# A two-layer graph network kernel: set-up and loop in one block, weights folded by whole fp32 products

## The reference, cut to what matters

```python
# x [128, 128, 256] f32, adj [128, 128, 128] int
h = relu(layernorm(x));  A = (adj != 0)
for i in range(3):                      # a gated graph layer, weights shared but for weight[i]
    m = h @ weight[i]                   # [256, 256]
    aggr = einsum('bst,bsd->btd', A, m)
    gi = aggr @ w_ih.T + b_ih           # w_ih, w_hh [768, 256]
    gh = h @ w_hh.T + b_hh
    r, z = sigmoid(i_r + h_r), sigmoid(i_z + h_z)
    n = tanh(i_n + r * h_n)
    h = (1 - z) * n + z * h
x = x + h
h = relu(layernorm(x))
Wh = h @ W.T;  s1 = Wh @ a1;  s2 = Wh @ a2      # attention layer
att = softmax(where(adj == 0, -inf, leaky_relu(s1[:, :, None] + s2[:, None, :])))
out = x + att @ Wh
```

## Time and profile before

| what | value |
|---|---|
| median of three runs | 1756.61 us |
| the profiled execution, its own time | 1757.19 us |
| its span, first to last instruction | 1755.4 us |
| PE busy | 1737.4 us, 99% |
| DVE busy | 1491.1 us, 85% |
| ACT busy | 1104.0 us, 63% |
| POOL busy | 312.2 us, 18% |
| first gate product on PE | 36.22 us |

### The profile page before, as it was taken

How to read it: one execution, slowest core, us unless ns; L and a number is a source line. 1 busy time by engine, 2 the same in 40 slices (tenths; PEclk the granted TensorE clock), 3 DMA queues, 4 the chain that set the end, 5 groups by cost and what they waited for, 6 DMA issues and landing times. The chain is left out here.

```text
span 1755.4 us, 32032 instructions
## 1 busy us (share of the span) xinstructions
PE 1737.4 (99%) x10108; PEld 906.8 (52%) x10108; DVE 1491.1 (85%) x2916; ACT 1104.0 (63%) x2005; POOL 312.2 (18%) x759
## 2 busy tenths in 40 slices
PE   7999999999999999999999999999999999999998
PEld 5444555545555454554545555455554545545455
DVE  6578898888988888888888988889888888888888
ACT  5456666666566666666666666665666666666664
POOL 1022022210212112021120222102121120211200
PEclk9999999999999999999999999999999999999999
DMA  4334352354424444253343523444244342533332
GB/s 116 71 61 103 59 133 55 72 119 89 114 42 103 94 84 108 42 120 87 74 114 62 129 54 74 117 90 114 42 106 91 84 108 42 120 88 73 79 67 67
DMA packets 395712, 152.03 MB, mean 87 GB/s; under 512 B 307360, under 2 KB 391840, under 8 KB 395680
## 3 DMA queue, kind: packets, MB, share of 16 engines
q1 hardware_dynamic: 395680, 151.64, 38.4%
HBM read 60.83 MB, written 16.84 MB: 44 GB/s over the span
## 5 line engine op out<-in xcount | busy, mean ns | idle before, releaser
L1162 ACT ACTIVATE n_out<-n_pre,bih 128x512 f32<-128x512 f32 x192 | 137.8, 718 | 191.7 <-DVE n_pre L1286 190.8
L551 ACT ACTIVATE nb_hi<-nb_bank 128x512 f16<-128x512 f32 x192 | 114.0, 594 | 217.4 <-PE nb_bank L537 217.4
L522 PE MATMUL hn_bank<-ht_s,wh_hi 128*128 128x512 f16 x768 | 228.4, 379 | 1.7 <-PEq L637 1.7
L522 PE MATMUL z_bank<-ht_s,wh_hi 128*128 128x512 f16 x768 | 228.4, 379 | 0.0
L522 PE MATMUL r_bank<-ht_s,wh_hi 128*128 128x512 f16 x768 | 228.4, 379 | 0.0
L1157 ACT ACTIVATE tanh_r<-r_bank,b_rz,down 128x512 f32<-128x512 f32 x192 | 148.5, 773 | 113.1 <-PE r_bank L522 113.1
L1281 DVE SCALAR_TENSOR_TENSOR n_pre<-tanh_r,hn_b 128x512 f32<-128x512 f32 x192 | 147.6, 769 | 79.2 <-ACT tanh_r L1157 77.0
L555 DVE TENSOR_TENSOR nb_lo<-nb_bank,nb_hi 128x512 f16<-128x512 f32 x192 | 131.1, 683 | 49.5 <-ACT nb_hi L551 49.5
L1529 POOL TENSOR_TENSOR ht<-ht_s 128x512 f32<-128x512 f16 x64 | 86.0, 1345 | 468.7 <-DMA ht_s<-h_s 350.5
L1152 ACT ACTIVATE hn_b<-hn_bank,b_hn,down 128x512 f32<-128x512 f32 x192 | 147.8, 770 | 19.0 <-PE hn_bank L522 18.9
L1166 ACT ACTIVATE tanh_z<-z_bank,b_rz,down 128x512 f32<-128x512 f32 x192 | 147.2, 767 | 18.8 <-PE z_bank L522 18.3
(11 more groups left out here) (258 smaller groups left out, 3786.3 us busy)
## 6 DMA issues: line engine op xcount, KB each, us to landing
x_in<-in_x_dram SPq DMA_DIRECT2D x32, 512.0 KB, 4.7
x_res<-in_x_dram SPq DMA_DIRECT2D x32, 512.0 KB, 4.3
out_dram<-x_out SPq DMA_DIRECT2D x30, 512.0 KB, 5.0
adj_in<-in_adj_dram SPq DMA_DIRECT2D x32, 256.0 KB, 5.4
adj_att<-in_adj_dram SPq DMA_DIRECT2D x32, 256.0 KB, 4.5
s_row<-s_dram SPq DMA_DIRECT2D x30, 256.0 KB, 3.6
h_s<-ht_s SPq DMA_TRANSPOSE x128, 3.1
ht_s<-h_s SPq DMA_TRANSPOSE x64, 3.3
```

What stands on the lines that cost most here:

```text
L522: last = nc.tensor.matmul(bank_ap, w, d, start=start and i == 0, stop=stop and i == len(todo) - 1)
L551: nc.scalar.activation(nb_hi[a][:, c, :], nb_bank[:], ACT.Copy).then_inc(nb_hi_ready, 1)
L1162: nc.scalar.activation(n_out[c][:], n_pre[c][:], ACT.Tanh, bias=bih[:, 4 + c:5 + c]).then_inc(n_ready, 1)
```

## The change

Set-up and loop become one block: `set_up_sync`, `set_up_gpsimd`, `set_up_tensor`, `set_up_scalar` and `set_up_vector` are called at the head of each engine's part, so an engine goes on to the loop when its own set-up items are done. The banks of the set-up are now those of the loop (hn 0, r 1, in 2, z 3, w 4, s 5), with waits at the first gates for the last fill of each. The temporary tiles lie where later tiles of the attention layer lie, so the first `load_att` waits for the last fill.

Each engine has its own written order (`SETUP`). `w_ih` and the layer weights are kept whole in fp32 after their transposes (`ih_t`, `w_t`), with no `lo` part, and a `wi` fill is two whole fp32 products in place of six fp32r ones. A refill of banks 0 to 5 that held fills 0 to 9 waits for ACT alone. Biases and attention vectors come in 16 contiguous rows by three DMAs and are turned by one PE transpose into `t_bank` (`turn_small`), which DVE copies out; `col` is no longer a fill but a step on PE early in the order, into `t_bank`, copied by ACT. The items of `HEAD` now follow the first hn step of pair 0.

```diff
-SETUP_SIDE = { ... }
+SETUP = {
+    "pe": [0, 1, ("turn_small",), 3, 2, ("col",), 4, 9, 5, 8, 7, 6, 11, 12, 10, 15, 14, 13, 16, 17, 18, 19,
+           ("neighbours", 0, 0), 21, 20, 22, 23, 24, 25, 27, ("neighbours", 0, 1), 26, 28],
+    "act": [0, 1, 2, 3, 4, 5, 6, 7, 8, 9, ("apply_gnn", 0), 11, 12, 13, 14, 15, 16, 17, 18, 19, 20, 21, ("col",), 22,
+            ("neighbours", 0, 0), 23, 24, 25, 26, ("neighbours", 0, 1), 27, 28],
+    "dve": [("bias",), ("peak", 3), ("stats", 0), ("peak", 0), ("peak", 1), ("peak", 2), ("stats", 1), 10,
+            ("adjacency", 0), 11, 12, ("split_gnn", 0), 13, 14, 15, 16, 17, 18, 19, 20, 21, ("neighbours", 0, 0),
+            ("adjacency", 1), 22, 23, 24, 25, ("neighbours", 0, 1), 26, 27, 28],
+    "pool": [("stats", 0), ("stats", 1)],
+    "sp": [("load_ih", 0), ("load_att",), ("load_ih", 1), ("load_small",), ("load_x",), ("load_w",), ("load_hh",),
+           ("load_group", 1), ("load_adj",), ("first_transpose", 0, 0), ("first_transpose", 0, 1)],
+}
-HEAD = [("apply_gnn", 1), ("split_gnn", 1), ("first_transpose", 1, 0), ("first_transpose", 1, 1)]
+FIRST_SLOT = {0: [("apply_gnn", 1), ("split_gnn", 1), ("first_transpose", 1, 0), ("first_transpose", 1, 1)]}
...
-                            pe.wait_ge(bank_read, 6 + KC * layer)
-                            last = products(bank[:, 0:cols.stop - cols.start],
-                                            [(w_hi[:, layer, e, k * P:(k + 1) * P], w_lo[:, layer, e, k * P:(k + 1) * P],
-                                              ih_hi[:, e, cols], ih_lo[:, e, cols]) for e in range(KC)])
+                    pe.wait_ge(hi_ready, 6 + KC * layer)
+                    for e in range(KC):
+                        last = nc.tensor.matmul(bank[:, 0:cols.stop - cols.start], w_t[:, layer, e, k * P:(k + 1) * P],
+                                                ih_t[:, e, cols], start=e == 0, stop=e == KC - 1)
...
+            def load_small():
+                sp.dma_start(rows[0:6, :], b_ih.rearrange("(c p) -> c p", p=P)).then_inc(loaded["small"], 16)
+                sp.dma_start(rows[6:12, :], b_hh.rearrange("(c p) -> c p", p=P)).then_inc(loaded["small"], 16)
+                sp.dma_start(rows[12:16, :], att_a.rearrange("o (c p) -> (o c) p", p=P)).then_inc(loaded["small"], 16)
...
+            def turn_small():
+                pe.wait_ge(loaded["small"], 48)
+                nc.tensor.transpose(t_bank[:, 0:16], rows[:], ident[0:16, 0:16]).then_inc(small_turned, 1)
...
+            def wait_read(engine, n):          # nested alike in the set-up
+                engine.wait_ge(hi_ready, n + 1) if n < transposed else engine.wait_ge(bank_read, read_by(n))
...
             @block.tensor
             def _(pe):
+                set_up_tensor(pe)
...
+                    if first_group(p, a) and layer == 0 and c == 0:
+                        if name == "z":
+                            pe.wait_ge(bank_read, read_by(len(fills) - 1))
+                        else:
+                            pe.wait_ge(bank_read, read_by(max(last_fill[GATE_BANK[name]], WEIGHTS_READ)))
```

More of the change, by code:

```diff
@@ new lines, in graph_blocks, with setup_order @@
+        fills += [("hh", k, part) for k in range(KC) for part in range(2)]
+        fills += [("wi", (2, k), part) for k in range(KC) for part in range(2)]
+        fills += [("att", k, 0) for k in range(KC)]
+        def setup_order(fill, side, order):
+            for item in order:
+                if isinstance(item, int):
+                    fill(item, *fills[item])
+                else:
+                    stage, *group = item
+                    side[stage](*group)
+        turns = [n for n in SETUP["pe"] if isinstance(n, int) and n != transposed]
@@ new lines, in filled, with read_by, split_target @@
+        def filled(n):
+            return turns.index(n) + 1
+        def read_by(n):
+            return n + 1 - transposed
+        def wait_read(engine, n):
+            if n < transposed:
+                engine.wait_ge(hi_ready, n + 1)
+            else:
+                engine.wait_ge(bank_read, read_by(n))
+        last_fill = {bank: max(n for n in range(len(fills)) if n % len(banks) == bank) for bank in range(len(banks))}
+        def split_target(what, where, which):
+            if what == "ih":
+                return ih_t[:, where, HALF[which]], None, 1.0
+            if what == "w":
+                layer, e = where
+                return w_t[:, layer, e, :], None, 1.0
+            if what == "hh":
+                return wh_hi[:, where, COLS[which]], wh_lo[:, where, COLS[which]], (up_n if which else up_rz)
+            if what == "att":
+                return wa_hi[:, where, :], wa_lo[:, where, :], up_att
+            layer, k = where
+            return wi_hi[:, layer, k, COLS[which]], wi_lo[:, layer, k, COLS[which]], up_in
@@ L842, in after_gates, with first_group @@
+        GATE_BANK = {"hn": 0, "r": 1, "in": 2, "z": 3}
+        WEIGHTS_READ = max(n for n, (what, where, _) in enumerate(fills) if what == "hh" or what == "wi" and where[0] == 0)
+        def first_group(p, a):
+            return isinstance(p, int) and p == 0 and a == 0
         def after_gates(p):
@@ L915, in slots @@
                     gate(p, slot % 2, slot // 2, STEPS[step][:-1], step // 4)
+                    for stage, *which in FIRST_SLOT.get(step, ()) if slot == 0 and not exists(p - 1) else ():
+                        if stage in side:
+                            side[stage](p, *which)
                     for stage, *which, offset in table.get((slot, step), ()):
@@ L942, in _ @@
             def _(sp):
+                set_up_sync(sp)
                 def store(p, a):
```

446 lines of the change are left out of this document (203 added, 243 removed).

## The result

The changed kernel takes 1752.55 us (median of 11 runs, 1751.95 to 1753.18) against 1756.61 us (11 runs, 1755.82 to 1757.66) of the kernel before in the same session: 4.06 us less, ratio 0.9975 with an interval of 0.9967 to 0.9984. The forecast was 1752.5. The profiled execution took 1753.15 with a span of 1751.4. Both are 4.0 under their counterparts of before (1757.19 and 1755.4).

A forecast was written before the change was run, and what follows sets the result against it. PE, gapless from its first gate product, bounds the kernel: dense work at 7.2, small transposes to 8.6, `col` to 12.05, w to 13.65, plus 18.5 puts that product at 32.15 against 36.22; 4.1 less, median 1752.5 us, range 1750.9 to 1755.0.

The forecast's parts named there:

- (a): Start of PE's dense work, when the small rows have landed: 7.2 us, with 6.0 and 9.0 as ends.
- (b): Six transposes of the small rows on PE at the slow pitch: 1.3 us, to 8.6.
- (c): The eight `col` instructions, now early on PE, at half speed: 3.44 us, to 12.05.
- (d): Twelve transposes of w on PE, whose speed rises to full at 12.65: done at 13.65, ends 13.3 and 14.0.
- rival 1: PE's speed rises at a fixed time, 15.8, whatever PE does: first gate 33.75, time 1754.1 us; chance 0.13.
- (e): PE from first whole product to first gate, all at full speed: 18.5 us, of which six weight pairs take 15.5.
- The cover: Slack of other engines' work behind PE: peaks 0.8 us, scales 1.2, read before first `hn` 0.6, group 1's state 2.3.
- 2: Small rows land late, at 10, shifting PE and DVE one for one: first gate 34.95, 1755.3 us; chance 0.08.
- 3: PE stays at half speed past fill 10: first gate 36.2, or 41.4 and 1761.8 us if it lasts; chance 0.04.
- 4: PE is ready before DVE's peaks (15.4), which set the end: first gate 31.35, 1751.7 us; chance 0.12.
- 5: Group 1 late for the first slot, or another start-up wait, eats 1 to 2 us: 1753.9 us; chance 0.08.
- The accounting behind the gain: Set-up's 4.9 us: -3.0 dearer products, +1.7 `col`, +1.7 barrier, +1.3 half-speed first products, +0.7 peaks wait, 2.5 other waits.

The follow-up runs named there:

- e5: The changed kernel measured again, unedited: 1752.87 us, 3.8 less than the kernel before.
- e6: The changed kernel with the three loads of the small rows issued behind the first x: 1754.71 us, 2.0 less than the kernel before.
- e4: The changed kernel with unused identity transposes on PE, twelve before fill 0 and four before `turn_small`: 1751.54 us, 6.0 less than the kernel before.
- e3: The changed kernel with `col` moved to the end of the set-up order, behind fill 28: 1755.40 us, 2.2 less than the kernel before.
- e1: The changed kernel with the first hn product waiting until DVE has read the last fill: 1757.02 us, 0.5 less than the kernel before.
- e7: The kernel of e1 with 26 unused identity transposes on PE ahead of the wait: 1755.48 us, 1.2 less than the kernel before.
- e8: The changed kernel with one fp32r product for each whole fp32 one, no low parts: 1751.31 us, 5.4 less than the kernel before.
- e2: The changed kernel with three fp32r products for each whole fp32 one, low parts not made: 1750.44 us, 7.1 less than the kernel before.
- e10: The kernel of e8 with 26 unused identity transposes on PE between fills 16 and 17: 1750.35 us, 6.7 less than the kernel before.
- e9: The kernel of e4 with fill 14 ahead of PE's peaks and DVE's second statistics behind fill 18: 1751.20 us, 5.9 less than the kernel before.
- e11: e2's products with e4's transposes, fill 14 ahead of the peaks, second statistics behind fill 25: 1749.99 us, 7.1 less than the kernel before.

## Why the prediction was right

Step by step, forecast and measured:

- (a) Dense work from 7.2: the rows were turned at 6.79 (6.55 in e5). 0.4 early, inside 6.0 to 9.0, and e6 shows it is worth one for one.
- (b) and (c) The transposes and `col` at the slow pitch: 8.6 to 12.05 forecast, 8.33 to 11.74 measured. 3.44 against 3.41: doubling the full-speed row was right.
- (d) The rise at 12.65 and fill 11 at 13.65: about 12.5 and 13.53. Moving the rise with the start of dense work was the choice that decided between the forecast and rival 1. e6 (work 1.7 later, rise 1.7 later), e4 (work earlier, rise near 7) and e3 (a gap of 1.65, rise near 14.0) rule out a fixed time, since 7, 13.4 and 14.0 all lie outside the 10.8 to 12.5 of the unedited order. What I did not see is how loose it is: the same order has fill 11 at 13.53 and 12.96, and with the same work ahead of it e1 and e7 have 12.68 and 12.63. All of them lie below my value, and three of the four below the 13.3 that I gave as the early end. The value that I took was hit by the one profile with the latest rise.
- (e) 18.5 from fill 11 to the first gate: 18.69. A whole product of 512 columns was not in the trace and I doubled the one of 256: 0.43 per instruction and 1.72 per fill in both ways of counting. Of the 0.19 too little, 0.12 lie in the first fill (1.79 for 1.72) and in the last (0.91 for 0.86). The Trainium skill ("FP8 and Floating Point Precision", "TensorE Precision Notes") counts a true fp32 product as four passes; as an estimate from this count, whole products would cost 1.33 of three fp32r ones. Measured it is 1.22 (2.58 to 2.11), and the first gate by that estimate, 33.35, is 1.1 past the measured one. The whole product does agree with the count: 0.43 for 256 columns is four times 0.108, half of the 0.215 that an fp16 product of 512 columns takes. It is the fp32r product that takes more than that, 0.117.
- The cover: peaks ready 15.4 forecast, 14.62 measured, so 1.6 of cover and not 0.8; tops 16.9 and 16.82; first bank read 20.6 and 20.62; the read that the first `hn` waits for 31.4 and 31.00, 1.2 before PE's start and not 0.6 (which by the prediction's own sum, 32.15 less 31.4, is 0.75). `tanh_r` +5.3 and +5.39, group 1 split +6.7 and +6.8. Nothing became late.
- The first gate at 32.15: 32.22. The span 1751.3: 1751.4. The execution 1753.1: 1753.15. Some of this closeness is luck: (a) was taken 0.4 too late and (e) 0.2 too short, and the rise alone moves fill 11 by 0.9 between profiles. e5, with nothing changed, has its first gate at 31.66 and a span of 1750.8. The medians, 1752.55 and 1752.87, are the firmer hit.

The rivals: 1 fell with e6, e4 and e3. 2 is a true mechanism whose condition was not met, and e6 shows its price. 3, half speed past fill 10, did not come; but the fall of the speed itself exists, after idling, as e1 and e8 show, and I had not listed it. 4 is true in e4; its numbers were off, since the peaks are ready at 14.5 and not 15.4, so that it gives 1751.54 and a first gate at 30.59, and not 31.35. So "nothing gives more than this without quicker loads" was too strong. 5 did not come: no gap in the first slot.

The accounting behind the gain was only partly tested. The cost of the products (2.4 to 2.8 of the 3.0) and the place of `col` (1.7) are shown. That PE gains by not waiting for the copies is shown by e1 and e7: in e7 the wait takes 2.9 (31.32 to 34.23), and 2.6 of the gain of 3.8 is gone. The term in the prediction is another, the 1.7 of the old order, and was not tested alone; neither were the 2.5 for other waits. The 1.3 us for the first products at half speed and the 0.7 for the peaks were only argued from the trace.

## What to carry to other kernels

Where the main engine is gapless after the set-up, find its first instruction of the main stretch and measure what moves that: here the end followed it within 0.3 us in eleven of the twelve profiles of the table. Before trading dear instructions for cheap ones, look whether the engine will then stand idle: cheaper products (e8) gave less than dearer ones (e2), as the idling cost speed as well. Where TensorE is the bound and has to wait, try filling the wait with work that nobody needs: here the work behind it then ran at full speed, and at the start of the kernel it gave 1.9 to 2.2 us by the differences from before (e4).

## What the runs showed of the hardware

- After 2.74 us of idling (e1) and 2.65 (e8) PE fell to half speed, for 3.3 and some 5.6 us, with granted clocks of 0.66 and 0.50 in those stretches; in e1 the first two products behind the wait were still at full speed. After 1.68 us it did not fall. Filled with transposes (e7, e10) the same waits cost no speed. The Trainium skill, "TensorE: Matmul & The Clock Gate", Part 1, says that recent activity sets the clock and that half rate is the default; the traces agree, and the start of e4 too.
- In the first 12 us of the changed kernel PE's pitch is that of half speed (0.43 for a `col` instruction) while the granted clock is printed as 1.00, the third number from the end of this line; after the falls it is printed as 0.50 and 0.66. At a start the pitch, not that column, tells the speed.

```profile
4.00:12.00 8.00, 6.73 (x23) 5.50 (x24) 4.83 (x11) 1.85 (x4) 2.03 (x10) 1.00 1.08 350
```

- The same work does not raise the speed at the same moment: between about 10.8 and 12.5 in the seven traces that begin alike (the changed kernel's two, e1, e2, e7, e8, e10), worked out from the step at which the pitch halves. That may be a good part of the spread of 1.2 to 1.6 us between runs of the changed kernel, which is 0.14 when PE is busy from 1.67 us on (e4). It is not shown: e9 and e11 start PE as early and span 0.83 (5 runs) and 0.64 (4), with w's landing at 10.0 to 10.7 as another thing that varies, and only the profiled execution of each kernel has a trace of its rise.
- A whole fp32 product of 256 columns costs 0.43 us, three fp32r ones 0.35, at full speed.
